# Rotated cross attention in a four-layer decoder: the keys' projection moves into the layer before, the inverse roots to ScalarE, all rotations to VectorE

## The chip, the cores and the metric

One core of one Trainium2 chip runs the whole kernel. The metric is the device time of one execution in microseconds. Its matrix engine is TensorE (PE in the profile, PEld for its weight loads), its vector engine VectorE (DVE), its activation engine ScalarE (ACT), the general one GpSimd (POOL); SyncE (SP) issues the transfers. SBUF is the on-chip memory, PSUM the accumulators that TensorE writes, eight banks of 512 fp32 per partition.

## The reference

The reference is a decoder on x of shape (8, 128, 128): eight sequences of 128 positions and 128 features. It has four layers, each of self attention, cross attention to a context and a feed-forward part. The change is in the first layer's cross attention, with 16 heads of 8 features:

```python
x = x + _L0_attn_ref(_layernorm(x), ...)
# cross attention: q from the normalized x, k and v from ctx_1024
q = rope(rms_norm(heads(_layernorm(x) @ Wq.T), q_norm_w))
k = rope(rms_norm(heads(ctx @ Wk.T), k_norm_w))
v = heads(ctx @ Wv.T)
x = x + (softmax(q k^T * 8**-0.5) v) @ Wo.T
# rms_norm over the 8 features of a head, eps 1e-10; rope turns
# feature i and i+4 of a head by the cosine and sine of its position
```

The keys and values depend on the context alone, so they can be computed before x is ready. The block ahead of it (L0a, the first layer's self attention) is a gated, quantized recurrence: x is normalized, rounded, multiplied by ternary weights, passed through an exponential, a logarithm and another exponential, normalized and rounded again, and projected.

## The kernel before

The eight sequences are held in two groups of four (g is 0 and 1). Each group has its own SBUF tiles and its own four PSUM banks. The program of each engine is written once per group as a generator that yields a pair (layer, phase) ahead of each piece of work; `weave` always runs the piece with the smallest pair, group 0 first on a tie. So the phase numbers fix the order of the instructions on each engine, and nothing is reordered on the chip. Engines wait for each other by semaphores (`wait_ge` on a named step). The layers are named L0a (attention), L0x (cross attention), L0f (feed-forward) and so on.

In L0a, VectorE computes the sums of the recurrence (L1362), then two mean squares per group (L1369 to L1373, "ms1" and "ms2"), whose inverse roots GpSimd takes as a power (L327, one instruction per group and root), and then the scales of the rounding (L1386 to L1392). After that come the transposes (L429), ScalarE's copy to bf16 (L929), the clamp (L1395), the projection and the residual sum into x (L1400).

In L0x:
- PE waits for x of L0a, projects keys into bank 1 and values into bank 2 from the transposed context (16 matmuls), transposes the normalized x and projects the queries.
- ACT copies the values (L867) and the transposed x (L856), squares queries and keys (L935) and copies the raw keys to the tile td (L856).
- DVE sums the squares per head (L1411), and takes the inverse roots of queries and keys together, 128 numbers per partition, by a shift, a constant and three rounds of Newton's method (L1413 to L1424, twelve instructions per group). It scales the queries (L1427) and rotates them (L1180, L1183 twice, L1185) into tc.
- POOL scales the keys (L356) and rotates them (L361, L363 twice, L365) into td, beside DVE.
- PE transposes both (L429), ACT copies them to QT and KT (L856), and the first masked keys are made by DVE (L1208) and POOL (L341).

Then the attention runs in 8 units per group: PE writes the mask (L413, ps<-bt) and the scores (L413, ps<-KTm,qk), DVE takes maxima (L1220) and subtracts (L1226), PE transposes (L476), ACT takes exponentials (L876), PE multiplies by the values. The code that the change touches:

## Time and profile before

| quantity | value |
|---|---|
| median of three runs | 748.72 us (747.66 to 748.99) |
| profiled execution | 747.51 us, of which its span is 745.7 us |
| mean granted clock of TensorE | 0.887 of full speed |
| PE busy | 597.0 us (80%) |
| DVE busy | 474.7 us (64%) |
| ACT busy | 249.3 us (33%) |
| POOL busy | 119.3 us (16%) |
| chain that ended last | PE 69%, DVE 23%, POOL 4%, ACT 2%, issue 2% |

The busy time of an engine is an average over stages of very different kinds; the chain names, at each moment, the work for which everything later waited. The granted clock has two levels, 0.5 (1.2 GHz) and 1.0 (2.4 GHz). The stretch around the change runs from 45 to 105 us of the span.

### The profile page before, as it was taken

What the parts mean: (1) busy time and instruction counts of PE and PEld (TensorE: products, weight loads), DVE (VectorE), ACT (ScalarE), POOL (GpSimd) and SP (SyncE); (2) the same over time, 40 slices, a digit from 0 to 9 for tenths busy, and PEclk for the clock granted to TensorE, in tenths of its full rate; (3) what the DMA queues carried; (4) which work ended last, traced back from release to release, by engine and by line L of the source; (5) the groups of instructions that cost most, each with busy time, mean ns of one, the idle gap of its engine ahead of it and who ended that gap; (6) DMA issues with size and microseconds to landing.
All of it is one profiled execution on the core that took longest, in us unless ns stands there. A gap on an engine that the chain in (4) does not pass through costs nothing.

```text
span 745.7 us, 10768 instructions
## 1 busy us (share of the span) xinstructions
PE 597.0 (80%) x4297; PEld 391.0 (52%) x4297; DVE 474.7 (64%) x1212; ACT 249.3 (33%) x371; POOL 119.3 (16%) x118
## 2 busy tenths in 40 slices
PE   1414599977899889969987679999779958998567
PEld 1314255667455646556765646456435654556425
DVE  7788867677587567754344634875554455876585
ACT  2342124415334333424323342344221022443261
POOL 5022611013220041000002014100200043102020
PEclk9657579979899999997998899999799986999879
DMA  9700000000000000000000000000000000000000
GB/s 298 304 0 1 0 1 1 2 1 2 0 1 2 1 1 2 1 1 1 1 0 1 1 0 1 1 2 1 1 0 1 0 1 0 2 1 1 1 0 29
DMA packets 6721, 12.41 MB, mean 17 GB/s; under 512 B 528, under 2 KB 4880, under 8 KB 6288
## 3 DMA queue, kind: packets, MB, share of 16 engines
q1 hardware_dynamic: 6672, 11.73, 4.4%
q8 instruction: 34, 0.56, 0.3%
q14 instruction: 15, 0.12, 0.1%
HBM read 11.21 MB, written 0.52 MB: 16 GB/s over the span
## 4 chain that ended last, share of the span: by engine, by line
PE 69%; DVE 23%; POOL 4%; ACT 2%; issue 2%; DVEq 0%; ACTq 0%; POOLq 0%
PE ps L413 52%; PE ps L476 11%; PE ps L429 3%; DVE st L1121 2%; PE ps L495 2%; DVE xn L1309 2%; POOL rs L327 2%; DVE mx L1220 2%; DVE big L1226 2%; DVE mv L1124 1%; DVE x L1239 1%; PE ps L585 1%; ACT big L876 1%; DVE big L1451 1%; DVE s L1449 1%
## 5 line engine op out<-in xcount | busy, mean ns | idle before, releaser
L1220 DVE TENSOR_REDUCE mx<-ps 128x8 f32<-128x1024 f32 x80 | 98.0, 1224 | 58.8 <-PE ps L413 58.7
L876 ACT ACTIVATE big<-ps 128x1024 f32<-128x1024 f32 x80 | 81.9, 1024 | 129.3 <-PE ps L476 129.3
L1226 DVE TENSOR_TENSOR big<-ps,mx 128x1024 f32<-128x1024 f32 x80 | 98.0, 1225 | 6.9
L476 PE MATMUL ps<-kt,big 128*128 128x128 f32 x640 | 90.9, 287 | 7.0 <-DVE big L1226 6.9
L413 PE MATMUL ps<-KTm,qk 32*128 32x512 f32 x320 | 95.6, 677 | 0.0
L327 POOL TENSOR_TENSOR rs<-ve,negh 128x4 f32<-128x4 f32 x26 | 26.6, 1024 | 411.7 <-DVE ve L1126 411.6
L476 PEld LDWEIGHTS ps<-kt,big 128*128 128x128 f32 x640 | 71.4, 145 | 35.0 <-DVE big L1226 18.5
L413 PE MATMUL ps<-xnT,wt 128*128 128x512 f32 (+1 forms) x148 | 78.8, 672 | 3.1 <-DVE big L1496 3.1
L413 PEld LDWEIGHTS ps<-wt,big 128*128 128x128 f32 (+1 forms) x480 | 56.0, 191 | 9.2 <-issue 9.1
L413 PE MATMUL ps<-wt,big 128*128 128x128 f32 (+1 forms) x480 | 59.8, 279 | 0.0
L413 PEld LDWEIGHTS ps<-big,vaug 128*32 128x32 f32 x1280 | 30.4, 109 | 48.0 <-ACT big L876 45.5
L341 POOL TENSOR_TENSOR KTm<-qk,kt 128x512 f32<-128x512 f32 x34 | 37.6, 1114 | 104.4 <-PE ps L413 93.4
L413 PE MATMUL ps<-big,vaug 128*32 128x128 f32 x1280 | 50.5, 278 | 0.0
L413 PE MATMUL ps<-bt 128*128 128x512 bf16 (+1 forms) x192 | 48.6, 364 | 0.0
L429 PE MATMUL ps<-kt,xn 128*128 128x128 f32 x80 | 18.4, 373 | 36.9 <-DVE xn L1309 36.5
L413 PEld LDWEIGHTS ps<-xnT,wt 128*128 128x128 f32 (+1 forms) x148 | 29.4, 214 | 32.4 <-issue 27.3
L856 ACT ACTIVATE xnT<-ps 128x512 f32<-128x512 f32 x30 | 17.9, 598 | 80.1 <-PE ps L429 69.8
L413 PEld LDWEIGHTS ps<-KTm,qk 32*128 32x128 f32 x320 | 25.4, 194 | 35.4 <-issue 32.5
L1285 DVE SCALAR_TENSOR_TENSOR x<-ps,gw,x 128x128 f32<-128x128 f32 x80 | 22.3, 344 | 30.3 <-PE ps L413 29.5
L413 PEld LDWEIGHTS ps<-wt,xnT 128*128 128x128 f32 x256 | 37.4, 232 | 3.3 <-issue 2.7
L413 PE MATMUL ps<-wt,xnT 128*128 128x128 f32 (+2 forms) x256 | 37.6, 308 | 0.2 <-ACT xnT L856 0.2
L429 PEld LDWEIGHTS ps<-kt,xn 128*128 128x128 f32 x80 | 12.0, 187 | 41.7 <-issue 31.1
(273 smaller groups left out, 783.4 us busy)
## 6 DMA issues: line engine op xcount, KB each, us to landing
wt<-in_weights SPq DMA_DIRECT2D x1, 1664.0 KB, 17.0
wt<-in_weights SPq DMA_DIRECT2D x1, 1603.0 KB, 11.9
wt<-in_weights SPq DMA_DIRECT2D x6, 256.0 KB, 11.2
bt<-in_bconsts SPq DMA_DIRECT2D x1, 1024.0 KB, 8.5
rowt<-in_rows SPq DMA_DIRECT2D x1, 975.0 KB, 6.6
wt<-in_weights SPq DMA_DIRECT2D x1, 832.0 KB, 13.5
wt<-in_weights SPq DMA_DIRECT2D x1, 608.0 KB, 18.0
wt<-in_weights SPq DMA_DIRECT2D x1, 580.0 KB, 5.5
```

The lines of the kernel that those rows point to most:

```text
L327: pool.tensor_tensor(out, src, negh[:, :], ALU.pow).then_inc(*s.step(name + "_r"))
L341: pool.tensor_tensor(t.KTm[:, b % 2, :, :], keys_of(t, b), own_head(), ALU.mult).then_inc(*s.step(f"keys{b}"))
L413: return pe.matmul(out, lhsT, rhs, start=start, stop=stop, **k)
L429: ins = pe.transpose(seq(bk, b), src[:, b, :], ident)
L476: ins = pe.transpose(heads_of(pair(g, u))[:, j // HG, j % HG, :], pr[:, (u % 2) * HH + j, :], ident)
L495: ins = pe.transpose(out, t.ot[b][:, i * P:(i + 1) * P], ident)
L856: act.activation(out, src, ACT.Copy).then_inc(*s.step(name))
L876: act.activation(half, heads_of(pair(g, u)), ACT.Exp, scale=SCALES[l]).then_inc(*s.step(f"exp{u}"))
L1121: dve.bn_stats(t.st[:, b, :], src[:, b, :]).then_inc(*s.step())
L1220: dve.tensor_reduce(top, S, AX.X, ALU.max).then_inc(*s.step())
L1226: dve.tensor_tensor(pr[:, half * HH:(half + 1) * HH, :].rearrange("p (i j) k -> p i j k", i=2), S, top.unsqueeze(3).to_broadcast([P, 2, HG ...
L1285: dve.scalar_tensor_tensor(x[:, b, :], bank(banks[e])[:, b * P:(b + 1) * P], gw[:, b, e:e + 1], x[:, b, :], ALU.mult, ALU.add).then_inc(*s ...
```

## The change

The changed kernel moves the key projection of L0x into the end of L0a, at phase 12.5, into bank 2. It waits there for the step ms1, after which bank 2 has been read. ACT squares and copies the raw keys there as well, and DVE sums the squares. In L0x the value projection waits only for that copy instead of for x. The inverse roots are computed by ACT as exp(-0.5 * ln(sum/8 + 1e-10)), one logarithm and one exponential per group for the keys (phase 0.2 and 0.4) and for the queries (phase 6). DVE rotates the keys too: group 0's ahead of the queries, group 1's after them. The queries are rotated from PSUM first and scaled afterwards. Group 0's keys are transposed early; the others at their old place. POOL waits for both groups' rotated queries before it spreads keys. The first masked keys are made at phase 7 instead of 19. The last attention layer (L3a) keeps its form. Declarations of a constant and of tiles are cut from the diff.

```diff
...
@@ -335,2 +337,5 @@
                         pool.wait_ge(*s.at(f"{l}.KT"))
+                        if l == "L0x":
+                            for other in range(GROUPS):
+                                pool.wait_ge(*s.at("L0x.qrot", other))
                         if first == 0:
@@ -352,10 +357,3 @@
                 pool.wait_ge(*s.at(f"{l}.kraw"))
-                if l == "L0x":
-                    pool.wait_ge(*p.at("pre.gwT"))
-                    pool.wait_ge(*s.at("L0x.y2"))
-                    pool.tensor_tensor(raw, new, t.y2[:, heads:2 * heads].unsqueeze(2).to_broadcast([P, heads, HD]), ALU.mult).then_inc(*s.step())
-                    pool.wait_ge(*s.last())
-                    cos, sin, one, two = cw[1][:, :], sw[1][:, :], slice(0, HD // 2), slice(HD // 2, HD)
-                else:
-                    cos, sin, one, two = const("c3"), const("s3"), slice(0, HD, 2), slice(1, HD, 2)
+                cos, sin, one, two = const("c3"), const("s3"), slice(0, HD, 2), slice(1, HD, 2)
                 pool.tensor_tensor(new, raw, cos.unsqueeze(1).to_broadcast([P, heads, HD]), ALU.mult).then_inc(*s.step())
@@ -391,3 +389,3 @@
                     rsqrt(t.rs[:, :], t.ve[:, :], "var2")
-                if l in ("L0x", "L3a"):
+                if l == "L3a":
                     yield from rotate_keys(n, l)
@@ -542,2 +540,8 @@
+            def turn_keys():
+
+                pe.wait_ge(*s.at("L0a.x"))
+                pe.wait_ge(*s.at("L0x.krot"))
+                turn_rows(1, t.td, "KTp")
+
             def turn_gates(n, l, k):
@@ -566,4 +570,3 @@
                     if l == "L0x":
-                        pe.wait_ge(*s.at("L0a.x"))
-                        project_rows(1, ctxT, w("L0x_wk"), "k")
+                        pe.wait_ge(*s.at("L0a.kraw"))
                     else:
@@ -602,4 +605,9 @@
                         pe.transpose(bank(3)[:, 0:E2], gwn[:, :], ident[0:E2, 0:E2]).then_inc(*p.step("gwTp"))
-                    yield n, 14
+                    yield n, 12.5
                     pe.wait_ge(*s.at("L0a.ctxT"))
+                    if g == 0:
+                        pe.wait_ge(loaded["L0x"], 16)
+                    pe.wait_ge(*s.at("L0a.ms1"))
+                    project_rows(2, ctxT, w("L0x_wk"), "k")
+                    yield n, 14
                     if g == GROUPS - 1:
@@ -621,2 +629,5 @@
                         project_rows(2, xnT, w("L3a_wv"), "v")
+                    if l == "L0x" and g == 0:
+                        yield n, 6
+                        turn_keys()
                     yield n, 8
@@ -624,4 +635,7 @@
                     turn_rows(0, t.tc, "QTp")
-                    pe.wait_ge(*s.at(f"{l}.krot"))
-                    turn_rows(1, t.td, "KTp")
+                    if l == "L3a":
+                        pe.wait_ge(*s.at("L3a.krot"))
+                        turn_rows(1, t.td, "KTp")
+                    elif g == GROUPS - 1:
+                        turn_keys()
                     yield n, 20
@@ -863,2 +877,14 @@
+            def logarithm(m, need):
+
+                part = slice(m * GB * H, (m + 1) * GB * H)
+                act.wait_ge(*s.at(need))
+                act.activation(t.y2[:, part], t.v2[:, part], ACT.Ln, bias=tiny[:, 0:1], scale=1.0 / HD).then_inc(*s.step("log"))
+
+            def inverse_root(m, name):
+
+                part = slice(m * GB * H, (m + 1) * GB * H)
+                act.wait_ge(*s.last())
+                act.activation(t.y2[:, part], t.y2[:, part], ACT.Exp, scale=-0.5).then_inc(*s.step(name))
+
             def values():
@@ -897,2 +923,6 @@
                 if l == "L0x":
+                    yield n, 0.2
+                    logarithm(1, "L0a.kv")
+                    yield n, 0.4
+                    inverse_root(1, "kroot")
                     yield n, 1
@@ -924,2 +954,6 @@
                     act.activation(tc[:, :, :], tc[:, :, :], ACT.Exp, scale=-float(P)).then_inc(*s.step("f128"))
+                    yield n, 12.5
+                    act.wait_ge(*s.at("L0a.k"))
+                    act.activation(t.ta[:, GB:2 * GB, :], four(bank(2)), ACT.Square).then_inc(*s.step("ksq"))
+                    read(t.td[:, :, :], four(bank(2)), "k", "kraw")
                     yield n, 13
@@ -932,6 +966,7 @@
                     if l == "L0x":
-                        for m, nm in ((1, "k"), (0, "q")):
-                            act.wait_ge(*s.at(f"L0x.{nm}"))
-                            act.activation(t.ta[:, m * GB:m * GB + GB, :], four(bank(m)), ACT.Square).then_inc(*s.step(f"{nm}sq"))
-                        read(t.td[:, :, :], four(bank(1)), "k", "kraw")
+                        act.wait_ge(*s.at("L0x.q"))
+                        act.activation(t.ta[:, 0:GB, :], four(bank(0)), ACT.Square).then_inc(*s.step("qsq"))
+                        yield n, 6
+                        logarithm(0, "L0x.qv")
+                        inverse_root(0, "qroot")
                     if l == "L3a":
@@ -940,4 +975,7 @@
                     yield n, 9
+                    if l == "L0x" and g == 0:
+                        read(KT, bank(1), "KTp", "KT")
                     read(QT, bank(0), "QTp", "QT")
-                    read(KT, bank(1), "KTp", "KT")
+                    if l == "L3a" or g == GROUPS - 1:
+                        read(KT, bank(1), "KTp", "KT")
                     yield from attend(n, l)
@@ -1174,2 +1212,7 @@
+            def mean_of_heads(m, name):
+
+                part = t.v2[:, m * GB * H:(m + 1) * GB * H]
+                dve.tensor_reduce(part, ta[:, m * GB:m * GB + GB, :].rearrange("p b (h d) -> p (b h) d", h=H), AX.X, ALU.add).then_inc(*s.step(name))
+
             def rotate(v, cos, sin, out, name, swap):
@@ -1187,2 +1230,6 @@
+            def first_keys(l):
+                dve.wait_ge(*s.at(f"{l}.KT"))
+                dve.tensor_tensor(t.KTm[:, 0, :, :], keys_of(t, 0), own_head(), ALU.mult).then_inc(*s.step("keys0"))
+
             def attend(n, l):
@@ -1204,6 +1251,5 @@
-                if l in ("L0x", "L1a", "L3a"):
+                if l in ("L1a", "L3a"):
                     yield n, 19
-                    dve.wait_ge(*s.at(f"{l}.KT"))
-                    dve.tensor_tensor(t.KTm[:, 0, :, :], keys_of(t, 0), own_head(), ALU.mult).then_inc(*s.step("keys0"))
+                    first_keys(l)
                 if l in ("L1x", "L2x"):
@@ -1383,2 +1429,5 @@
                     variance_of(outer, 1e-8, "ms2")
+                    yield n, 12.5
+                    dve.wait_ge(*s.at("L0a.ksq"))
+                    mean_of_heads(1, "kv")
                     yield n, 13
@@ -1403,28 +1452,25 @@
                 if l == "L0x":
+                    def rotate_keys():
+                        raw = ta[:, GB:2 * GB, :].rearrange("p b (h d) -> p (b h) d", h=H)
+                        dve.wait_ge(*s.at("L0x.kroot"))
+                        dve.tensor_tensor(raw, td[:, :, :].rearrange("p b (h d) -> p (b h) d", h=H),
+                                          wide(t.y2[:, GB * H:2 * GB * H], HD), ALU.mult).then_inc(*s.step())
+                        dve.wait_ge(*s.last())
+                        rotate(raw, cw[1][:, :], sw[1][:, :], td, "krot", "half")
-                    v2, y2, h2, hh = t.v2, t.y2, t.h2, GB * H
+                    if g == 0:
+                        yield n, 2
+                        rotate_keys()
                     yield n, 6
-                    dve.wait_ge(*s.last())
-                    for m, nm in ((0, "q"), (1, "k")):
-                        dve.wait_ge(*s.at(f"L0x.{nm}sq"))
-                        v = ta[:, m * GB:m * GB + GB, :].rearrange("p b (h d) -> p (b h) d", h=H)
-                        dve.tensor_reduce(v2[:, m * hh:(m + 1) * hh], v, AX.X, ALU.add).then_inc(*s.step())
-                    dve.wait_ge(*s.last())
-                    dve.tensor_scalar(v2[:, :], v2[:, :], 1.0 / HD, 1e-10, ALU.mult, ALU.add).then_inc(*s.step())
-                    dve.wait_ge(*s.last())
-                    dve.tensor_scalar(h2[:, :].bitcast(I32), v2[:, :].bitcast(I32), 1, None, ALU.logical_shift_right).then_inc(*s.step())
-                    dve.wait_ge(*s.last())
-                    dve.tensor_scalar(y2[:, :].bitcast(I32), h2[:, :].bitcast(I32), -1.0, float(0x5F3759DF), ALU.mult, ALU.add).then_inc(*s.step())
-                    dve.wait_ge(*s.last())
-                    for _ in range(3):
-                        dve.tensor_tensor(h2[:, :], y2[:, :], y2[:, :], ALU.mult).then_inc(*s.step())
-                        dve.wait_ge(*s.last())
-                        dve.scalar_tensor_tensor(h2[:, :], h2[:, :], -0.5, v2[:, :], ALU.mult, ALU.mult).then_inc(*s.step())
-                        dve.wait_ge(*s.last())
-                        dve.scalar_tensor_tensor(y2[:, :], h2[:, :], 1.5, y2[:, :], ALU.add, ALU.mult).then_inc(*s.step("y2"))
-                        dve.wait_ge(*s.last())
-                    v = ta[:, 0:GB, :].rearrange("p b (h d) -> p (b h) d", h=H)
-                    dve.tensor_tensor(v, bank(0).rearrange("p (h d) -> p h d", d=HD), wide(y2[:, 0:hh], HD), ALU.mult).then_inc(*s.step())
-                    dve.wait_ge(*s.last())
-                    rotate(v, cw[0][:, :], sw[0][:, :], tc, "qrot", "half")
+                    dve.wait_ge(*s.at("L0x.qsq"))
+                    mean_of_heads(0, "qv")
+                    yield n, (6.2 if g == 0 else 6.4)
+                    rotate(bank(0).rearrange("p (h d) -> p h d", d=HD), cw[0][:, :], sw[0][:, :], tc, "qraw", "half")
+                    dve.wait_ge(*s.at("L0x.qroot"))
+                    new = tc[:, :, :].rearrange("p b (h d) -> p (b h) d", h=H)
+                    dve.tensor_tensor(new, new, wide(t.y2[:, 0:GB * H], HD), ALU.mult).then_inc(*s.step("qrot"))
+                    if g == GROUPS - 1:
+                        rotate_keys()
+                    yield n, 7
+                    first_keys(l)
                 if l == "L3a":
```

**VectorE, where L0x begins.** The first fence is the kernel before, from group 1's normalized x to the end of the first Newton round of group 0; v2, h2 and y2 are sums, half values and roots, and the last digit is the group.

```order
L1309 TENSOR_SCALAR xn1<-x1,mv1,rs1 128x128 x4
L1411 TENSOR_REDUCE v20<-big0 128x64 x2
L1413 TENSOR_SCALAR v20<-v20 128x128
L1415 TENSOR_SCALAR h20<-v20 128x128
L1417 TENSOR_SCALAR y20<-h20 128x128
L1420 TENSOR_TENSOR h20<-y20 128x128
L1422 SCALAR_TENSOR_TENSOR h20<-h20,v20 128x128
L1424 SCALAR_TENSOR_TENSOR y20<-h20,y20 128x128
```

Two more such rounds, the scaling and the rotation of the queries follow, and then all of it again for group 1. The changed kernel has from the same place on (cw1 and sw1 are the cosines and sines of the keys, cw0 and sw0 those of the queries):

```order
L1355 TENSOR_SCALAR xn1<-x1,mv1,rs1 128x128 x4
L1456 TENSOR_TENSOR big0<-td0,y20 128x512
L1223 TENSOR_TENSOR td0<-big0,cw1 128x512
L1226 TENSOR_TENSOR big0<-big0,sw1 128x64x4 x2
L1228 TENSOR_TENSOR td0<-td0,big0 128x512
L1216 TENSOR_REDUCE v20<-big0 128x64
L1216 TENSOR_REDUCE v21<-big1 128x64
L1223 TENSOR_TENSOR tc0<-ps,cw0 128x512
L1226 TENSOR_TENSOR big0<-ps,sw0 128x64x4 x2
L1228 TENSOR_TENSOR tc0<-tc0,big0 128x512
L1471 TENSOR_TENSOR tc0<-tc0,y20 128x512
L1223 TENSOR_TENSOR tc1<-ps,cw0 128x512
```

The twelve small instructions of each group are gone; four instructions of group 0's key rotation and its scaling stand in front of the queries' sums. Group 1's keys come behind group 1's queries:

```order
L1226 TENSOR_TENSOR big1<-ps,sw0 128x64x4 x2
L1228 TENSOR_TENSOR tc1<-tc1,big1 128x512
L1471 TENSOR_TENSOR tc1<-tc1,y21 128x512
L1456 TENSOR_TENSOR big1<-td1,y21 128x512
L1223 TENSOR_TENSOR td1<-big1,cw1 128x512
L1226 TENSOR_TENSOR big1<-big1,sw1 128x64x4 x2
L1228 TENSOR_TENSOR td1<-td1,big1 128x512
L1233 TENSOR_TENSOR KTm0<-qk0,kt 128x512
L1233 TENSOR_TENSOR KTm1<-qk1,kt 128x512
```

What moved is the whole key rotation, from POOL to DVE, and the scaling of the queries, from ahead of the rotation to behind it.

**ScalarE, from the end of L0a to the transposed keys.** Before, from the last rounding on (the semaphore each waits for is in brackets):

```order
L929 ACTIVATE qk0<-ps,magic 128x512 [waits L0a_tensor0]
L929 ACTIVATE qk1<-ps,magic 128x512 [waits L0a_tensor1]
L867 ACTIVATE vaug0<-ps 128x64x8 [waits L0x_tensor0]
L867 ACTIVATE vaug1<-ps 128x64x8 [waits L0x_tensor1]
L856 ACTIVATE xnT0<-ps 128x512 [waits L0x_tensor0]
L856 ACTIVATE xnT1<-ps 128x512 [waits L0x_tensor1]
L935 ACTIVATE big0<-ps 128x512 [waits L0x_tensor0] x2
L856 ACTIVATE td0<-ps 128x512 [waits L0x_tensor0]
L935 ACTIVATE big1<-ps 128x512 [waits L0x_tensor1] x2
L856 ACTIVATE td1<-ps 128x512 [waits L0x_tensor1]
L856 ACTIVATE qk0<-ps 128x512 [waits L0x_tensor0] x2
L856 ACTIVATE qk1<-ps 128x512 [waits L0x_tensor1] x2
```

In the changed kernel from the copy of group 1's transposed x on:

```order
L870 ACTIVATE xnT1<-ps 128x512 [waits L0x_tensor1]
L968 ACTIVATE big0<-ps 128x512 [waits L0x_tensor0]
L968 ACTIVATE big1<-ps 128x512 [waits L0x_tensor1]
L882 ACT_TABLE_LOAD
L882 ACTIVATE y20<-v20,tiny 128x64 [waits L0x_vector0]
L888 ACT_TABLE_LOAD
L888 ACTIVATE y20<-y20 128x64 [waits L0x_scalar0]
L882 ACT_TABLE_LOAD
L882 ACTIVATE y21<-v21,tiny 128x64 [waits L0x_vector1]
L888 ACT_TABLE_LOAD
L888 ACTIVATE y21<-y21 128x64 [waits L0x_scalar1]
L870 ACTIVATE qk0<-ps 128x512 [waits L0x_tensor0] x2
```

Each logarithm and each exponential has a table load ahead of it; the loads themselves carry no wait. The keys' roots stand ahead of the value copies: a load, the logarithms of both groups, a load, the exponentials of both groups.

**TensorE, from the gate transposition in L0a.** Before:

```order
L602 MATMUL ps<-kt,gwn 128x16
L429 MATMUL ps<-kt,big0 128x128 x4
L429 MATMUL ps<-kt,big1 128x128 x4
L413 MATMUL ps<-wtern,qk0 128x128 x4
L413 MATMUL ps<-wtern,qk1 128x128 x4
L413 MATMUL ps<-wt,ctxT0 128x128 x8
L413 MATMUL ps<-wt,ctxT1 128x128 x8
```

After:

```order
L605 MATMUL ps<-kt,gwn 128x16
L411 MATMUL ps<-wt,ctxT0 128x128 x4
L411 MATMUL ps<-wt,ctxT1 128x128 x4
L427 MATMUL ps<-kt,big0 128x128 x4
L427 MATMUL ps<-kt,big1 128x128 x4
L411 MATMUL ps<-wtern,qk0 128x128 x4
L411 MATMUL ps<-wtern,qk1 128x128 x4
L411 MATMUL ps<-wt,ctxT0 128x128 x4
L411 MATMUL ps<-wt,ctxT1 128x128 x4
```

Four matmuls per group, the key projection, moved from behind x of L0a to ahead of the last transposes of L0a.

## Rows read from the trace of the kernel before

**Rows 1.** The page: busy time by engine; the copies of ScalarE.
```profile
PE 597.0 (80%) x4297; PEld 391.0 (52%) x4297; DVE 474.7 (64%) x1212; ACT 249.3 (33%) x371; POOL 119.3 (16%) x118
...
L856 ACT ACTIVATE xnT<-ps 128x512 f32<-128x512 f32 x30 | 17.9, 598 | 80.1 <-PE ps L429 69.8
```

**Rows 2.** Chain of waits, 0:160; columns: start us, us, what.
```profile
88.35 5.83 PE ps L413 x12
94.19 1.90 PE ps L476 x8
...
98.94 1.90 PE ps L476 x8
...
104.02 2.06 PE ps L413 x22
106.08 1.03 PE ps L476 x8
```

**Rows 3.** Timeline of DVE, 43:100; columns: start, us, engine, line, operation, [idle before].
```profile
45.73 0.17 DVE L1373 TENSOR_SCALAR s<-s 128x4 f32<-128x4 f32 x1
...
49.42 0.17 DVE L1373 TENSOR_SCALAR s<-s 128x4 f32<-128x4 f32 x1
49.81 0.16 DVE L1386 TENSOR_TENSOR s<-s,s4b 128x4 f32<-128x4 f32 x1 [0.22 <-POOL s4b L327]
```

**Rows 4.** Timeline of DVE, further on: normalization, roots and rotation of group 0.
```profile
60.96 2.36 DVE L1309 TENSOR_SCALAR xn<-x,mv,rs 128x128 f32<-128x128 f32 x8
66.09 1.28 DVE L1411 TENSOR_REDUCE v<-big 128x64 f32<-128x512 f32 x2 [2.76 <-ACT big L935]
...
71.12 0.69 DVE L1427 TENSOR_TENSOR big<-ps,y 128x512 f32<-128x512 f32 x1
71.85 1.03 DVE L1180 TENSOR_TENSOR tc<-big,cw 128x512 f32<-128x512 f32 x1
72.80 2.23 DVE L1183 TENSOR_TENSOR big<-big,sw 128x256 f32<-128x256 f32 x2
...
76.08 1.28 DVE L1411 TENSOR_REDUCE v<-big 128x64 f32<-128x512 f32 x2
```

**Rows 5.** Timeline of PE, 43:100.
```profile
51.80 1.09 PE L429 MATMUL ps<-kt,big 128*128 128x128 f32 x4 [15.48 <-DVE big L1160]
...
57.40 5.62 PE L413 MATMUL ps<-wt,ctxT 128*128 128x128 f32 x32 [0.64 <-DVE x L1400]
62.85 1.19 PE L429 MATMUL ps<-kt,xn 128*128 128x128 f32 x8
64.19 2.05 PE L413 MATMUL ps<-wt,xnT 128*128 128x128 f32 x16 [0.15 <-ACT xnT L856]
```

**Rows 6.** Timeline of ACT, 36:45.
```profile
41.76 1.28 ACT L924 ACT_TABLE_LOAD   x1
43.06 1.15 ACT L924 ACTIVATE tc<-tc 128x512 f32<-128x512 f32 x2
```

**Rows 7.** Timeline of POOL, 43:100: the first operation of a key rotation.
```profile
71.26 1.07 POOL L356 TENSOR_TENSOR big<-td,y 128x512 f32<-128x512 f32 x1 [9.09 <-DVE y L1424]
```

**Rows 8.** Timeline of DVE, 590:640: a rotation in the last attention layer.
```profile
605.60 0.69 DVE L1180 TENSOR_TENSOR tc<-ps,kt 128x512 f32<-128x512 f32 x1 [2.99 <-PE ps L413]
606.20 0.75 DVE L1183 TENSOR_TENSOR big<-ps,kt 128x256 f32<-128x256 f32 x2
606.99 0.69 DVE L1185 TENSOR_TENSOR tc<-tc,big 128x512 f32<-128x512 f32 x1
```

**Rows 9.** Timeline of ACT, 600:622.
```profile
618.51 1.28 ACT L876 ACT_TABLE_LOAD   x1
```

**Rows 10.** Stretches; columns: window, length, busy PE PEld DVE ACT POOL, PEclk, DMA share, GB/s.
```profile
57.50:61.00 3.50, 3.50 (x17) 3.50 (x18) 3.40 (x23) 0.00 (x0) 1.01 (x1) 0.50 0.03 7
61.50:66.50 5.00, 4.59 (x38) 4.00 (x36) 2.11 (x8) 3.50 (x8) 0.67 (x1) 1.00 0.00 0
```

**Rows 11.** Line L959: small exponentials on ACT, ns min/median/max.
```profile
L959 ACT ACTIVATE lgm<-lgm x4: 222/226/231, 161.6 to 343.0; 128x32 f32<-128x32 f32 x2, 128x24 f32<-128x24 f32 x2
```

6 lines of the change are left out of this document (4 added, 2 removed).

## The prediction

> **What bounds the kernel now.** I read the page first: PE is the busiest engine with 597.0 us, DVE has 474.7 us [rows 1]. That says nothing of the stretch that is changed, so the chain of waits came next, and there I looked for the last moment that the change can move. It is 88.35 us, the end of the last key transposition, after which PE works without a pause into the attention [rows 2]. Everything behind it is in the same order in both kernels, so what the change gives is the shift of this one point, unless the clock of PE changes what follows. Then the timeline of each engine between 45 and 88 us, to see what each wait ends on. DVE finishes the normalized x at 63.32 us (60.96 + 2.36), sits idle 2.76 us for ScalarE's squares, starts group 0's roots at 66.09 and group 1's at 76.08, so a group costs 9.99 us of DVE, and two take it to 86.1 [rows 4]. Two transpositions of 1.12 us close the gap to 88.35 [rows 2]. DVE therefore bounds the stretch; PE and ACT wait for it.
>
> **A group's 9.99 us before.** The sums of squares take 1.28 us for two tensors. From 67.40 (the row of 66.09 plus its 1.28 and the handoff) to 71.12 run the twelve Newton instructions, 3.75 us. The scaling is 0.69 us, and from 71.85 to 76.08 the rotation takes 4.23 us [rows 4]. The same rotation in the last attention layer, from 605.60 to 607.68, takes 2.08 us, with 0.75 us for the two half products that take 2.23 us here [rows 4, 8]. The difference of 2.15 us falls in the time in which POOL rotates the keys, which starts at 71.26 [rows 7]. I read it as the two engines hindering each other in SBUF.
>
> **What is added in L0a.** PE sat idle 15.48 us until 51.80, so the key projection has room there [rows 5]. It may start at 45.9, when group 0's ms1 is written [rows 3]. Sixteen matmuls (32 records) took 5.62 us from 57.40; eight took 2.05 us from 64.19, 0.26 us each [rows 5]. The clock was 0.50 until 61.0 and 1.00 from 61.5 [rows 10]. With 1.8 us of the 5.62 at 0.26 us, nine matmuls are left for 3.8 us at the low clock, 0.43 us each. Four cost 1.7 us, so group 1's keys are there at 49.4. ACT's square takes 0.6 us (598 ns for the same copy) [rows 1], to 50.1. DVE has ms2 at 49.59 and its next instruction stood at 49.81 [rows 3]. Now two sums of 0.64 us come between. The second waits until 50.1 at most, and ends at 50.95. So L0a ends 1.16 us later. At the high clock it would be 1.1 us, with 0.6 us per matmul 1.9 us. ACT's four instructions end by 50.8, before 51.80, when the first rounded tile was transposed [rows 5].
>
> **What leaves L0x's front.** The values are projected while DVE adds x, and PE no longer carries the keys. This gives nothing by itself: the normalized x ends at 63.32 and its last transposition could hardly end sooner than it did, 62.85 + 1.19 = 64.04 [rows 4, 5]. The key roots stand on ACT before the value copies: two loads of 1.28 us and four small activations of 0.25 us (226 ns for 24 to 32 numbers) [rows 6, 11], 3.6 us. ACT can begin them when its last copy of L0a is done, which was before 57.40, and is 1.16 us later now, and so ends them by 62.2. The first transposed x comes at 64 or later: free.
>
> **The new path through DVE**, with 0.03 us between instructions. It starts 1.16 us late, at 64.5.
> - Group 0's keys: scaling 0.72, rotation 2.1 (the price of rows 8, since POOL does nothing in this stretch), to 67.35. Under it PE transposes x (to 65.1), ACT copies (to 65.8), PE projects both groups' queries (to 66.2 and 67.2), ACT squares them (66.9 and 67.85).
> - The queries' sums: 0.65 each, 68.0 and 68.7. They no longer wait, so the 2.76 us of idleness is filled.
> - Rotation of group 0's queries from PSUM: to 70.8. Meanwhile ACT takes the root. Its table load needs no operand, and in the last layer a load ran right behind the copy at 617.90, ahead of its exponential's wait [rows 9]. So: load from 67.9 to 69.2, logarithm 69.45, load 70.75, exponential 71.0. DVE waits 0.3 us, scales to 71.8.
> - Group 1's queries: rotation to 73.9, root at 71.0 + 2 x 1.55 = 74.1, scaling to 74.9.
> - Group 1's keys: 2.85 us, to 77.75. POOL may spread group 0's second keys from 75 on, one operation of about 1.1 us. Its four operations cost DVE 2.15 us in some 5 us, so I add 0.55, to 78.3. The ends are 0 and 1.1.
> - One transposition of 1.12 us: 79.5 instead of 88.35.
>
> The Trainium skill, page "SBUF — State Buffer", section "Who interferes with whom", says that of a DVE instruction with two SBUF inputs and a GpSimd one that reads SBUF, the one issued second blocks for the other's whole length. By it the last term could be 1.1 instead of 0.55 us; the trace agrees as far as two half products took 2.23 us beside POOL and 0.75 without.
>
> **The sum.** Before, from the normalized x: 2.77 + 9.99 + 9.98 + 2.24 = 25.0 us. After: 15.0 us. Less 10.0, plus 1.16 in L0a: 8.8 us less. The profiled execution took 747.51 us, so it becomes 738.7. The median of the three runs, 748.72, lies 1.2 us above, which gives **739.9 us**.
>
> **Rivals.**
> 1. *The queries are projected at the low clock.* Before, PE had worked from 57.40 without a pause when the clock rose about 61.2 [rows 5, 10]. Now it has only eight matmuls and then a gap of 2 us. If the clock stays low, the last transposition costs 0.5 us more and the projections 1.7 us each instead of 1.0, so group 1's squares come at 69.65, and its sums end at 70.3 instead of 68.7: 1.6 us later at the end, 741.5 us. For it speaks the gap, against it that 4 us of work still stand ahead of it.
> 2. *The clock in the attention.* There a unit cost 4.75 us (94.19 to 98.94) at first, and 3.09 us (2.06 + 1.03) later [rows 2]. The change to the fast rate came about 14 us after 88.35. One unit earlier gives 1.65 us more: 738.2.
> 3. *The halves cost that much without POOL too.* Then the layout, halves of four read from SBUF, and not the neighbour is what makes the rotation slow. The key rotations would cost 4.25 each: 4.3 us more, 744.2 us. Against it: the last sum of a rotation has the same layout in both layers, and took 1.0 us here (75.03, the end of the half products, to 76.05) and 0.69 us there [rows 4, 8].
> 4. *A table switch costs twice its row.* It would be 2.6 us each if it also had to wait for the engine to drain. The queries' roots then come at 73.6 and 79.3, the keys' end moves to 83.5 and the transposition to 84.6: only 3.75 us less, 745.0. Against it: from the load at 41.76 to the exponential at 43.06 lie 1.30 us [rows 6]. The Trainium skill, page "ScalarE: Activation LUTs", section "What ACT_TABLE_LOAD costs", states 1283 ns and a drain of about 1380 ns for every switch; by its figure an estimate of the whole is this rival's. The load's own length agrees with the trace, a drain is not seen there.
> 5. *Slower than before: the attention stays at the low clock.* The place is the first units of the scores. The transposes that precede them now come scattered, at 67, 72, 75 and 78 us, with DVE's work between. If the clock rose not after three cold units but later, each one costs 1.65 us. From six more units (9.9 us) on, the kernel is slower than before; with eight it is 753 us. For it: before, PE was busy in all of 88 to 102 and the clock still stayed low. Against it: those units themselves did raise it, and they are unchanged.
>
> **How the numbers follow.** My forecast 0.58, rival 1 0.16, rival 2 0.11, rival 3 0.05, rival 4 0.05, rival 5 0.03, a gain lost in other ways 0.02. Two parts in a thousand, 1.5 us, are about what a measurement of this kernel can tell from no change. All but the last two are beyond that: faster 0.95, within it 0.02, slower 0.03. The range goes from 737.6 (a unit earlier, no contention) to 743.0 (rival 1 with both dear ends, 0.7 in L0a and 0.55 at POOL); rivals 3 to 5 lie outside.
>
> **What would show it.** In the changed trace: the first L0a scale instruction about 1.2 us later; no idleness of DVE ahead of the queries' sums beyond 0.1 us; all rotations near 2.1 us; ACT's load, logarithm, load, exponential in 3.1 us per group; the first mask matmul at 79.5. Wrong would be a DVE wait for ACT of more than 1 us at the scaling, half products over 0.5 us with POOL idle, or a start of the attention after 82.

## The result and the profile after

The changed kernel takes 739.36 us (738.49 to 741.1 in 4 runs) against 748.19 us (746.02 to 748.99) of the kernel before in the same comparison: a ratio of 0.9889, with a 95% interval of 0.9861 to 0.9918. The prediction was 739.9 us. The profiled execution took 739.54 us with a span of 737.7 us, 8.0 us less than before; the prediction had 738.7 us for it. Busy time went from DVE (474.7 to 468.7 us) and POOL (119.3 to 107.7) to ACT (249.3 to 259.2), as the page shows:

```profile
PE 597.4 (81%) x4289; PEld 392.3 (53%) x4297; DVE 468.7 (64%) x1198; ACT 259.2 (35%) x385; POOL 107.7 (15%) x109
```

The chain of waits around the start of the attention (start us, us, what) answers to [rows 2]:

```profile
79.68 1.09 PE ps L427 x4
80.77 5.84 PE ps L411 x12
86.61 1.90 PE ps L474 x8
...
91.37 1.90 PE ps L474 x8
...
95.24 1.03 PE ps L474 x8
...
98.33 1.02 PE ps L474 x8
```

The start of the attention stands at 80.77 instead of 88.35, 7.6 us earlier. This execution was already 0.26 us later than the one of before when group 0's ms1 was written, which lies ahead of everything that the change touches (45.99 against 45.73 in [rows 3]), so the change moved the start by 7.8 us; 8.8 were predicted. From there on the two are alike: a unit costs 4.76 us (86.61 to 91.37) at first and 3.09 us (95.24 to 98.33) later, and the fast rate comes 13 to 14 us after the start in both.

DVE after the change answers to [rows 3] and [rows 4] (start, us, engine, line, operation, count, idle before it and what ended it):

```profile
49.76 0.68 DVE L1216 TENSOR_REDUCE v<-big 128x64 f32<-128x512 f32 x1
50.74 0.69 DVE L1216 TENSOR_REDUCE v<-big 128x64 f32<-128x512 f32 x1 [0.30 <-ACT big L957]
51.34 0.15 DVE L1435 TENSOR_TENSOR s<-s,s4b 128x4 f32<-128x4 f32 x1
...
64.60 0.69 DVE L1456 TENSOR_TENSOR big<-td,y 128x512 f32<-128x512 f32 x1
...
68.05 1.51 DVE L1216 TENSOR_REDUCE v<-big 128x64 f32<-128x512 f32 x2 [0.64 <-ACT big L968]
...
72.17 0.69 DVE L1471 TENSOR_TENSOR tc<-tc,y 128x512 f32<-128x512 f32 x1 [0.62 <-ACT y L888]
...
75.40 0.69 DVE L1471 TENSOR_TENSOR tc<-tc,y 128x512 f32<-128x512 f32 x1 [0.55 <-ACT y L888]
76.01 0.69 DVE L1456 TENSOR_TENSOR big<-td,y 128x512 f32<-128x512 f32 x1
76.73 1.41 DVE L1223 TENSOR_TENSOR td<-big,cw 128x512 f32<-128x512 f32 x1
```

The path is the predicted one, with four kinds of small loss on it: the sums in L0a (the scale instruction stands at 51.34 instead of 49.81), a wait of 0.64 us for ScalarE's squares ahead of 68.05, one wait for each root, and one product of 1.41 us that takes 0.69 elsewhere. Beside that product POOL spreads the first keys:

```profile
76.27 1.33 POOL L346 TENSOR_TENSOR KTm<-qk,kt 128x512 f32<-128x512 f32 x1 [12.73 <-ACT qk L870]
```

ScalarE's roots of the queries, with table loads as long as those of [rows 6] and [rows 9]:

```profile
68.25 0.60 ACT L968 ACTIVATE big<-ps 128x512 f32<-128x512 f32 x1 [0.30 <-PE ps L411]
68.86 1.28 ACT L882 ACT_TABLE_LOAD   x1
70.16 0.35 ACT L882 ACTIVATE y<-v,tiny 128x64 f32<-128x64 f32 x1
70.52 1.28 ACT L888 ACT_TABLE_LOAD   x1
71.82 0.26 ACT L888 ACTIVATE y<-y 128x64 f32<-128x64 f32 x1
72.09 1.28 ACT L882 ACT_TABLE_LOAD   x1
```

A load lasts 1.28 us and the next activation starts 0.01 to 0.02 us behind it. A group costs 3.23 us (68.86 to 72.09), where the prediction had 3.1. The granted clock by stretch answers to [rows 10] (window, length, busy PE, PEld, DVE, ACT, POOL, granted clock, DMA share, GB/s):

```profile
57.80:61.00 3.20, 3.20 (x18) 3.20 (x16) 3.10 (x17) 3.16 (x7) 0.00 (x0) 0.50 0.03 8
61.00:66.50 5.50, 3.51 (x15) 2.81 (x15) 5.30 (x22) 1.94 (x4) 2.04 (x2) 0.50 0.00 0
66.50:71.00 4.50, 2.15 (x17) 1.91 (x16) 3.65 (x8) 3.30 (x5) 0.00 (x0) 0.95 0.00 0
```

Before, the clock was 1.00 from 61.5 to 66.5. Now PE has a pause of 1.86 us ahead of the first transposition of x (63.49), and its clock is 0.50 until 66.5.

### The profile page after: what moved, and what is told of

Read it like the earlier page. It is cut to its first block, busy times and chain, and to the rows that moved or that the text cites. A ratio compares the mean times of both kernels' runs of the same rounds, so it can differ in the third digit from the quotient of the medians.

```text
span 737.7 us, 10755 instructions
## 1 busy us (share of the span) xinstructions
PE 597.4 (81%) x4289; PEld 392.3 (53%) x4297; DVE 468.7 (64%) x1198; ACT 259.2 (35%) x385; POOL 107.7 (15%) x109
## 4 chain that ended last, share of the span: by engine, by line
PE 69%; DVE 20%; ACT 3%; POOL 3%; issue 2%; DMA 1%; SPq 1%; DVEq 0%; ACTq 0%
PE ps L411 52%; PE ps L474 11%; PE ps L427 3%; DVE st L1159 3%; PE ps L493 2%; DVE xn L1355 2%; POOL rs L329 2%; DVE big L1272 2%; DVE mx L1266 2%; DMA co<-in_ctx 1%; DVE mv L1162 1%; DVE x L1285 1%; PE ps L588 1%; ACT big L902 1%; DVE s L1495 1%
## 5 line engine op out<-in xcount | busy, mean ns | idle before, releaser
L411 PE MATMUL ps<-bt 128*128 128x512 bf16 (+1 forms) x184 | 46.9, 364 | 0.6 <-issue 0.2
L427 PEld LDWEIGHTS ps<-kt,xn 128*128 128x128 f32 x80 | 12.5, 194 | 44.2 <-issue 31.1
```

What stands on the lines that cost most here:

```text
L411: return pe.matmul(out, lhsT, rhs, start=start, stop=stop, **k)
L427: ins = pe.transpose(seq(bk, b), src[:, b, :], ident)
```

## The experiments

"Start" is the end of group 1's last key transposition, from which PE works on into the attention. The repairs of e5 to e8 move it by about a microsecond or less each, while the executions of one kernel differ by 2 to 11 us (737.42 to 739.29 in e5, 735.96 to 746.54 in e4). So the start and the local rows decide, and the totals are given beside them. Totals are medians, ratios are to the kernel before.

Each start is read from the one profiled execution of its kernel, and these executions differ ahead of the change as well. The last column takes that out: it is the start less the moment at which group 0's ms1 was written.

| kernel | profiled execution, us | ms1 of group 0 | start | start less ms1 |
|---|---|---|---|---|
| before | 747.51 | 45.73 | 88.35 | 42.62 |
| changed | 739.54 | 45.99 | 80.77 | 34.78 |
| e1 | 755.34 | 45.69 | 89.79 | 44.10 |
| e2 | 745.71 | 46.59 | 88.02 | 41.43 |
| e3 | 743.18 | 46.01 | 85.78 | 39.77 |
| e4 | 746.54 | 45.80 | 80.98 | 35.18 |
| e5 | 738.53 | 45.75 | 79.50 | 33.75 |
| e6 | 736.57 | 45.74 | 79.74 | 34.00 |
| e7 | 742.24 | 45.90 | 79.79 | 33.89 |
| e8 | 740.51 | 45.82 | 80.40 | 34.58 |
| e9 | 736.19 | 45.82 | 76.68 | 30.86 |
| e10 | 731.74 | 45.91 | 75.73 | 29.82 |
| e11 | 739.07 | 46.09 | 79.99 | 33.90 |
| e12 | 731.45 | 46.10 | 76.49 | 30.39 |

The profiled executions of e1 and e4 took 7 to 8 us more than their medians, those of e10 and e12 are the fastest of their kernels.

**e1: the move of the key rotation alone.** The kernel before, with POOL's scaling and rotation of the keys in L0x written on DVE behind the queries'.

```diff
-                if l in ("L0x", "L3a"):
+                if l == "L3a":
                     yield from rotate_keys(n, l)        # POOL
...
                     rotate(v, cw[0][:, :], sw[0][:, :], tc, "qrot", "half")
+                    dve.wait_ge(*s.at("L0x.kraw"))
+                    dve.tensor_tensor(raw, td..., wide(y2[:, hh:2 * hh], HD), ALU.mult).then_inc(*s.step())
+                    rotate(raw, cw[1][:, :], sw[1][:, :], td, "krot", "half")
```

> The kernel before with one part of the change: the key rotation of L0x moves from POOL to DVE, behind each group's query rotation; Newton roots and the late key projection stay. Theory (the slow rotations of before, 4.23 us, were due to POOL working beside them): every rotation now takes 2.1 us. A group costs DVE 1.28 + 3.75 + 0.72 + 2.1 + 2.85 = 10.7 us instead of 9.99, so the attention starts at about 88.7 us instead of 88.35, and the time is that of before, +0.3 us. Rival (the layout of halves read from SBUF is slow by itself): rotations stay near 4.2 us, the attention starts at about 97, +8 us.

Measured: 748.15 us, ratio 1.0019 (0.9984 to 1.0054); start at 89.8, where 88.7 was expected.

```profile
72.24 0.69 DVE L1180 TENSOR_TENSOR tc<-big,cw 128x512 f32<-128x512 f32 x1
72.85 0.75 DVE L1183 TENSOR_TENSOR big<-big,sw 128x256 f32<-128x256 f32 x2
73.63 0.69 DVE L1185 TENSOR_TENSOR tc<-tc,big 128x512 f32<-128x512 f32 x1
```

The same instructions in the same layout took 1.03, 2.23 and 1.0 us in [rows 4]. With POOL idle they are at the price of [rows 8]: the neighbour was the cause, and rival 3 falls. Each key rotation on POOL thus cost DVE 2.1 us in its own rotation, and one on DVE costs 2.85 us with its scaling, so the move alone gives nothing. The start is 1.1 us later than expected: a key spreading of POOL, from 79.05 to 80.16, stretched the Newton instruction issued at 79.30 from 0.29 to 1.01 us, and the queries' squares came 0.4 us later.

**e2: ScalarE's roots alone.** The kernel before with the twelve Newton instructions replaced.

```diff
-                    dve.tensor_scalar(v2[:, :], v2[:, :], 1.0 / HD, 1e-10, ALU.mult, ALU.add)...
...
+                        act.wait_ge(*s.at("L0x.sums"))
+                        act.activation(t.y2[:, :], t.v2[:, :], ACT.Ln, bias=tiny[:, 0:1], scale=1.0 / HD)...
+                        act.activation(t.y2[:, :], t.y2[:, :], ACT.Exp, scale=-0.5)...
```

> The kernel before with another part alone: the inverse roots of queries and keys by ACT (load, logarithm, load, exponential on 128 numbers per partition, per group), DVE waiting for them. Theory (a root costs DVE the wait, and DVE has nothing else to do in this order): group 0's first load can begin at 67.95 only, behind ACT's copies, so its root is there at 71.2, as late as Newton's; group 1's takes 2.0 us behind its sums instead of 3.75. The attention starts at about 86.6, -1.75 us against before. Rival (a switch of tables costs 2.6 us): start at 92 or later, +3 us.

Measured: 745.14 us, ratio 0.9962 (0.9938 to 0.9985); start at 88.0, which is 87.1 without the 0.9 us by which this execution was late ahead of the change; 86.6 was expected.

```profile
72.52 0.69 DVE L1422 TENSOR_TENSOR big<-ps,y 128x512 f32<-128x512 f32 x1 [4.02 <-ACT y L943]
73.25 0.96 DVE L1187 TENSOR_TENSOR tc<-big,cw 128x512 f32<-128x512 f32 x1
74.13 2.23 DVE L1190 TENSOR_TENSOR big<-big,sw 128x256 f32<-128x256 f32 x2
...
80.86 0.69 DVE L1422 TENSOR_TENSOR big<-ps,y 128x512 f32<-128x512 f32 x1 [2.16 <-ACT y L943]
```

In this order DVE waits 4.02 and 2.16 us for the roots that Newton's method took 3.75 us to make. The second wait is shorter since the load had run ahead of the logarithm's wait, as ScalarE's rows show:

```profile
72.44 1.28 ACT L941 ACT_TABLE_LOAD   x1
78.73 0.40 ACT L941 ACTIVATE y<-v,tiny 128x128 f32<-128x128 f32 x1 [5.01 <-DVE v L1418]
```

The half products are back at 2.23 us, with POOL beside them. A switch costs one load of 1.28 us (the logarithm that follows the load at 69.10 starts at 70.40), and rival 4 falls.

**e3: the queries' roots by Newton's method** in the changed kernel, twelve instructions on 64 numbers in place of `logarithm(0, ...)` and `inverse_root(0, ...)`:

```diff
-                        logarithm(0, "L0x.qv")
-                        inverse_root(0, "qroot")
...
                     mean_of_heads(0, "qv")
+                    ... 3 + 3 x 3 instructions on v2, h2, y2 [:, 0:GB * H]
```

> The changed kernel with the queries' roots by Newton on DVE again (twelve instructions on 64 numbers per partition, per group), the keys' roots still on ACT. Theory (with the sums in front, ACT's roots are hidden beside the rotations, and only waits of 0.6 us remained): 2 x 2.9 us of Newton come in, 1.17 us of waits go, the attention starts at 85.4 instead of 80.77, +4.6 us against the changed kernel. Rival (ACT's roots gave nothing, the gain came from the other parts): start within 1 us of 80.77.

Measured: 744.59 us, ratio 0.9958 (0.9923 to 0.9992); start at 85.8, 5.0 us later than in the changed kernel. The twelve instructions took 3.0 us (68.81 to 71.84); twice that is 6.0 us, less the waits for the roots. So 5.0 of the 7.8 us are that the queries' roots leave DVE *and* have a rotation to hide under: alone, the rotations on DVE (e1) made the start 1.5 us later and the roots on ScalarE (e2) 1.2 us earlier. The other 2.8 us belong to the rest of the change. By the rows, the early key projection gives DVE a key rotation to do where it was idle for 2.76 us, but no run takes that projection out alone, so its share is argued and not shown.

**e4: both key rotations on POOL**, in the changed order.

```diff
-                if l == "L3a":
+                if l in ("L0x", "L3a"):
                     yield from rotate_keys(n, l)        # POOL, after L0x.kroot
...
-                    if g == 0:
-                        yield n, 2
-                        rotate_keys()                   # DVE, and the same for the other group
```

> The changed kernel with both key rotations on POOL again, from the early roots of ACT (ready at 60.7). POOL is free from 63.5, so it turns group 0's keys to about 69.3 and group 1's to 75.1, while DVE has only the queries. Theory (a POOL rotation costs DVE about half of POOL's time while both work, and DVE waits for ACT anyway): the queries end near 76.8, two transpositions behind it, start of the attention at 79.0, 1.8 us better than the changed kernel. Rival (each query rotation costs 4.2 us again beside POOL): queries end at 78.6, start at 80.8, no difference.

Measured: 738.44 us, ratio 0.9852 (0.979 to 0.9914); start at 81.0, where 79.0 was expected. The rival had 80.8, from query rotations of 4.2 us. Both missed the mechanism:

```profile
62.23 4.81 DVE L1362 TENSOR_SCALAR xn<-x,mv,rs 128x128 f32<-128x128 f32 x8
```

The eight normalizations take 4.81 instead of 2.36 us. POOL starts on the keys at 63.41 and keeps at it; the normalizations ahead of that moment are at their usual 0.34 us, and the one issued at 64.48 takes 1.42 us. The queries' rotations, which ran later, were at 2.1 us even where POOL's last operation (71.90, 1.27 us) lay beside their first, which reads PSUM. DVE is rid of 5.7 us of key rotations, and now waits 3.5 us for the squares of the queries, which the later x holds back.

**e5: the sums over the squared keys late in L0a**, in DVE's gap ahead of the clamp; those of both groups, though the expectation of e9 speaks of group 1's.

```diff
-                    yield n, 12.5
-                    dve.wait_ge(*s.at("L0a.ksq"))
-                    mean_of_heads(1, "kv")
...
+                    yield n, 14.9
+                    dve.wait_ge(*s.at("L0a.ksq"))
+                    mean_of_heads(1, "kv")
```

> The changed kernel with the sums of the keys' squares on DVE moved from phase 12.5 of L0a to 14.9, into the gap in which DVE waits 0.28 and 1.30 us for ACT. Theory (in the changed kernel DVE's two sums and the wait for the second one put 1.5 us on the path of L0a: 49.81 became 51.34): they become free, the scale chain of L0a starts 1.3 us earlier and the attention at 79.4 instead of 80.77. Rival (the path of L0a's end runs through ACT's four key instructions or through PE): less than 0.5 us of it arrives.

Measured: 738.85 us, ratio 0.9858 (0.9814 to 0.9903); start at 79.5, 1.27 us earlier than in the changed kernel, or 1.03 us without what this execution was early ahead of the change.

```profile
49.83 0.16 DVE L1432 TENSOR_TENSOR s<-s,s4b 128x4 f32<-128x4 f32 x1 [0.22 <-POOL s4b L329]
...
53.69 1.27 DVE L1216 TENSOR_REDUCE v<-big 128x64 f32<-128x512 f32 x2
```

The scale instruction is back where [rows 3] has it, and the sums fill a gap. In L0a the repair is worth 1.27 us (from ms1 to the scale instruction it is 5.35 us in the changed kernel and 4.08 here); the start gets 1.03 of it. The term of L0a was real and avoidable.

**e6: both logarithms ahead of both exponentials**, one phase number each, and both rotations ahead of both scalings.

```diff
                         logarithm(0, "L0x.qv")
+                        yield n, 6.5
                         inverse_root(0, "qroot")
...
+                    yield n, 6.6
                     dve.wait_ge(*s.at("L0x.qroot"))
```

> The changed kernel with the queries' roots paired: logarithms of both groups behind one table load, then the exponentials of both behind another, and DVE rotates both groups' queries before it scales them. Two table loads fewer. Theory (DVE's waits of 0.62 and 0.55 us at the scaling come from ACT's four loads): both waits go, less one 0.03 gap; the attention starts 1.0 us earlier, at 79.8. Rival (the wait is ACT's handoff and not the loads): no difference.

Measured: 737.9 us, ratio 0.9858 (0.9809 to 0.9906); start at 79.7, 1.0 us earlier, or 0.8 us counted from ms1.

```profile
73.77 1.29 DVE L1473 TENSOR_TENSOR tc<-tc,y 128x512 f32<-128x512 f32 x2
```

ScalarE has two loads instead of four, and no wait stands at the scalings.

**e7: four needless matmuls after the values**, in PE's pause ahead of the normalized x.

```diff
                     project_rows(2, ctxT, w(f"{l}_wv"), "v")
+                    if l == "L0x" and g == GROUPS - 1:
+                        for b in range(GB):
+                            ins = mm(seq(3, b), ctxT[:, b * P:(b + 1) * P], w("L0x_wv"))
```

> The changed kernel with four more matmuls of PE behind group 1's value projection (the same products once more, into a bank that nobody reads before the next transposition overwrites it). They close PE's idle time of 1.86 us before the transposition of x. Theory (the queries were projected partly at the low clock because PE had stopped): the clock is at 1.0 before 63.5, the transpositions cost 0.6 and the projections 1.0 us each, ACT's second square ends near 67.6 instead of 68.85, and the attention starts 1.2 us earlier, at 79.5. Rival (the clock rises when it rises, or DVE's key rotation bounds this place anyway): start within 0.4 us of 80.77.

Measured: 739.26 us, ratio 0.9861 (0.9817 to 0.9905); start at 79.8, 1.0 us earlier, or 0.9 us counted from ms1.

```profile
65.21 2.01 PE L411 MATMUL ps<-wt,xnT 128*128 128x128 f32 x16
...
67.42 1.28 DVE L1220 TENSOR_REDUCE v<-big 128x64 f32<-128x512 f32 x2
```

The first row is PE's projection of the queries (2.56 us in the changed kernel), the second DVE's sums, of another answer of the same trace, now without a wait. The clock was 1.00 from 64 on here and 0.50 until 66.5 in the changed kernel. Needless work made the kernel's start earlier: rival 1's mechanism was at work in the changed kernel, at some 0.7 to 0.9 us.

**e8: POOL's first spread waits for group 1's rotated keys.**

```diff
                                 pool.wait_ge(*s.at("L0x.qrot", other))
+                            pool.wait_ge(*s.at("L0x.krot", 1))
```

> The changed kernel with one wait more: POOL spreads group 0's second keys only when group 1's keys are rotated. Theory (the one instruction of the rotation that took 1.41 instead of 0.69 us was held up by POOL's 1.33 us beside it): it takes 0.69 us, and the attention starts 0.7 us earlier, at 80.05. Rival (the 1.41 us is something of DVE's own): no difference.

Measured: 738.74 us, ratio 0.9855 (0.981 to 0.99); start at 80.4, where 80.05 was expected; counted from ms1 it is 0.2 us earlier than in the changed kernel and not 0.7. The queries' sums ended 0.3 us later, which the edit doesn't touch: PE projected the queries in 2.97 instead of 2.56 us, at a clock of 0.57 instead of 0.77 between 66 and 68.

```profile
77.08 0.69 DVE L1224 TENSOR_TENSOR td<-big,cw 128x512 f32<-128x512 f32 x1
```

The product is at 0.69 instead of 1.41 us. In the changed kernel it was issued at 76.73, while POOL's operation ran until 77.60, and ended at 78.14: it was held up for 0.72 of the 0.87 us that POOL had left. The Trainium skill, page "SBUF — State Buffer", section "Who interferes with whom", says that the later one waits until the earlier is through; this row agrees, nearly. The row of e10 does not show the whole length: there a sum issued at 71.19, when POOL's operation had 0.39 us left, paid 0.25 us.

**e9: all four together** (e5 to e8).

> All four repairs in one kernel: group 1's key sums late in L0a, both logarithms ahead of both exponentials, POOL's first spread after the rotated keys, and four matmuls between the values and the queries. Theory, that each loss was a term of its own on one path: the attention started at 80.77 in the changed kernel, less 1.27 (sums), 1.03 (logarithms), 0.98 (clock) and 0.72 (POOL), so it starts at 76.8, and the kernel takes 739.4 less 4.0, 735.4 us. Rival, that the repairs share a loss: the earlier x of the late sums makes ScalarE's squares or roots the last thing to come, and the start stays at 77.8 or later, 736.4 us or more.

Measured: 736.63 us, ratio 0.9873 (0.9844 to 0.9902). PE (start, us, engine, line, operation, count, idle before):

```profile
72.18 1.97 PE L428 MATMUL ps<-kt,tc 128*128 128x128 f32 x8 [5.42 <-DVE tc L1478]
75.59 1.08 PE L428 MATMUL ps<-kt,td 128*128 128x128 f32 x4 [1.45 <-DVE td L1234]
```

The start is at 76.7, 4.1 us earlier than in the changed kernel (3.9 from ms1), where 76.8 was expected and the rival had 77.8 or later. By the start the terms add up, and the rival falls. The time does not decide: it is 2.7 us less, not 4.0, and 736.63 us also meets the rival's 736.4 us or more. Six executions between 734.89 and 742.35 us can't tell the two apart.

**e10: e9, and group 1's keys rotated by POOL, after DVE's group 0.**

```diff
+                    pool.wait_ge(*s.at("L0x.kroot"))
+                    pool.wait_ge(*s.at("L0x.krot", 0))
...
-                if l == "L3a":
+                if l == "L3a" or l == "L0x" and g == GROUPS - 1:
                     yield from rotate_keys(n, l)        # POOL
```

> The combined kernel, and group 1's key rotation on POOL, begun only when DVE has rotated group 0's keys, so that no normalization or key work of DVE lies beside it. POOL's five operations take 1.2 us each, 6.0 us, from about 66 to 72.3, ahead of their use. DVE keeps only work on queries beside them, of which five instructions per group read PSUM or the table. Theory, that operands in PSUM keep DVE free of POOL: 2.85 us leave DVE's path and at most 0.5 per group come back at the last sum, so the attention starts at 74.2 to 74.9 instead of 76.8, and the kernel takes 732.8 to 733.5 us. Rival, that any DVE instruction that touches SBUF pays about 0.7 us beside POOL: five of them cost 3.5 us, the start stays at 77 or later, and nothing is gained over the combined kernel.

Measured: 732.71 us (731.74 to 735.54), ratio 0.9822 (0.9802 to 0.9843); start at 75.7.

```profile
67.29 0.68 DVE L1237 TENSOR_TENSOR tc<-ps,cw 128x512 f32<-128x512 f32 x1
67.89 0.75 DVE L1240 TENSOR_TENSOR big<-ps,sw 128x256 f32<-128x256 f32 x2
68.67 1.10 DVE L1242 TENSOR_TENSOR tc<-tc,big 128x512 f32<-128x512 f32 x1
```

With POOL busy from 66.23 to 71.58 beside them, the products that read PSUM are at their full speed (0.68 and 0.75 us), and the sum of two SBUF tiles pays 0.41 us, for group 1 0.25 us. That part of the theory is shown. But the start came only 1.0 us earlier than in e9, at 75.7 and not at 74.2 to 74.9. The chain of waits (start us, us, what) has PE in DVE's place now:

```profile
72.17 0.70 DVE tc L1486
72.92 2.82 PE ps L436 x12
```

All three sets of transpositions stand behind the scaling, at the low clock, 2.8 us; in e9 the two of the queries lay under DVE's key rotation. The time fell by 3.9 us, more than the start, and its 732.71 us meets the expected 732.8 to 733.5 by another cause than the expected one: the first units of the attention ran at the high clock:

```profile
76.00:80.00 4.00, 3.01 (x13) 0.75 (x11) 3.23 (x4) 0.37 (x1) 1.54 (x1) 1.00 0.00 0
```

**e11: PE's gaps ahead of the start filled**, in the changed kernel.

```diff
                         yield n, 6
                         turn_keys()
+                        for b in range(GB):
+                            for _ in range(2):
+                                ins = mm(seq(3, b), xnT[:, b * P:(b + 1) * P], w("L0x_wq"))
...                      # and the same behind group 0's turned queries
```

> The changed kernel with eight needless matmuls after the first keys' transposition and eight after group 0's queries', in PE's gaps of 4.3 and 2.2 us, so that PE works nearly without pause from 65.6 to 76. Their results are read by nothing. The attention starts at 80.8 as before, since DVE sets that. Question: what holds the clock at 0.50 in the attention's first 14 us. Theory, that it is the gaps ahead of the start: with them filled the clock is 1.00 at 80.8, three units cost 3.1 us instead of 4.75 and the first half unit as well, some 4.9 us less, 734.5 us. Rival, that the attention's own start (scores on 32 rows, with short pauses) holds it low whatever went before: the clock is 0.50 again a few us after 80.8, the gain is 0 to 1.5 us, 738 to 739.4 us.

Measured: 740.97 us, ratio 0.9919 (0.9903 to 0.9934); start at 80.0, where 80.8 was expected.

```profile
76.00:80.00 4.00, 1.75 (x12) 1.46 (x12) 3.84 (x6) 0.60 (x1) 1.27 (x1) 0.91 0.00 0
80.00:94.00 14.00, 14.00 (x40) 5.85 (x38) 8.04 (x7) 2.65 (x3) 2.59 (x2) 0.51 0.00 1
```

The clock was high up to the start and low right after it, for 14 us in which PE was busy all the time. As put, the theory falls and the rival holds. What the edit had left unfilled is the last pause, 2.25 us ahead of the last key transposition. This kernel with that pause filled as well was not run.

**e12: e9 with that last pause filled** by three matmuls.

```diff
                     elif g == GROUPS - 1:
+                        for b in range(GB - 1):
+                            ins = mm(seq(3, b), xnT[:, b * P:(b + 1) * P], w("L0x_wq"))
+                        ins.then_inc(*s.step("fill"))
                         turn_keys()
```

> The combined kernel with three needless matmuls between the queries' transpositions and group 1's keys', in the pause of 1.45 us that PE has there; at 0.43 us each they end at 75.4, so the start stays at 76.5 (up to 76.7). Their results are read by nothing. In the kernel with POOL rotating group 1's keys PE had no pause between 72.9 and 77.5, and the clock was 1.00 from about 76; in the combined kernel it paused from 74.15 to 75.59 and stayed at 0.50 to about 91.4. Theory, that this pause is what kept the clock down: it is 1.00 by 77 to 78, two to three units of 4.75 us become 3.1 us, and the kernel takes 736.6 less 3 to 5, 732 to 733.5 us. Rival, that something else decided it: the clock stays at 0.50 until 91 and the time is within 1 us of the combined kernel's, 736 to 737.5 us.

Measured: 733.2 us (731.45 to 738.59), ratio 0.9828 (0.9802 to 0.9854), 3.4 us less than e9, whose executions (734.89 to 742.35) and ratio (0.9844 to 0.9902) overlap with these; start at 76.5, as expected.

```profile
72.44 1.97 PE L428 MATMUL ps<-kt,tc 128*128 128x128 f32 x8 [5.42 <-DVE tc L1481]
74.21 1.48 PE L412 MATMUL ps<-wt,xnT 128*128 128x128 f32 x6
75.86 0.63 PE L428 MATMUL ps<-kt,td 128*128 128x128 f32 x4 [0.17 <-DVE td L1237]
76.33 0.59 PE L412 MATMUL ps<-bt 128*128 128x512 bf16 x2
76.85 1.13 PE L412 MATMUL ps<-KTm,qk 32*128 32x512 f32 x4
```

The transposition takes 0.63 instead of 1.08 us and the scores 1.13 instead of 2.08, from the first unit on. The clock and the median fit the theory, and the rival (0.50 until 91, 736 to 737.5 us) falls by the trace. That a pause there is what holds the clock down is not shown in general. The kernel before had none ahead of its last key transposition, and its clock stayed at 0.50 all the same:

```profile
86.11 1.12 PE L429 MATMUL ps<-kt,tc 128*128 128x128 f32 x4 [7.76 <-DVE tc L1185]
87.23 1.12 PE L429 MATMUL ps<-kt,td 128*128 128x128 f32 x4
```

Nor is the slow stretch behind the start of one length. By the granted clock it lasted 13 to 15 us in seven traces, but 8 us in e6, and 8.5 to 10 us in e1 to e4. In e6 the scores are fast from 88.0 on:

```profile
88.02 1.13 PE L411 MATMUL ps<-KTm,qk 32*128 32x512 f32 x4
```

e10 and e12 are the best versions found, some 14 us below the kernel before and 6 below the changed one.

## Why the prediction was right, point by point

- **The bound and the moment that moves.** Right. What the change gives is the shift of the start, 7.8 us, and the profiled executions differ by 8.0.
- **Rotations at 2.1 us without POOL** (rival 3 otherwise). Right, shown by e1.
- **A table switch costs its row** (rival 4 otherwise). Right, shown by e2 and by the four loads above. Its other half, that a load needs no operand, holds in e2 as well. The Trainium skill, page "ScalarE: Activation LUTs", section "What ACT_TABLE_LOAD costs", adds a drain of about 1380 ns; the load's 1.28 us agrees, and no row here shows the drain.
- **Sums in L0a: 1.16.** 1.27 us (51.34, less 0.26, less 49.81). e5 gives the 1.27 us back in L0a, and 1.03 us of it at the start.
- **Group 0's keys end at 67.35.** 67.41.
- **"They no longer wait" (the queries' sums).** This step failed in part. Predicted end 68.7, measured 69.48: a wait of 0.64 us, since PE transposed x and began to project the queries at the low clock, up to 66.5. Rival 1 had 70.3, so about half of it came true; e7 shows the mechanism. The argument against it, 4 us of work still ahead, weighed the work and not the pause of 1.86 us before it.
- **Waits for the roots, 0.3 and 0.2.** 0.62 and 0.55, some 0.4 us more at the end: the small logarithm took 0.35 us and not 0.25, and ScalarE's second square ended at 68.85 and not at 67.85.
- **POOL beside group 1's keys, 0.55 with ends 0 and 1.1.** 0.72 us on one instruction (e8).
- **Sum.** 79.5 predicted, 80.77 measured: 0.72 from the queries' squares, 0.38 from the roots, 0.16 from POOL, 0.10 from a later x (the execution's own offset of 0.26 us is more than that), less 0.09 in small differences.
- **The median came nearer than the path.** 739.36 against 739.9, though the path was 1.0 us longer than predicted. The profiled execution was 0.8 us above its forecast, and this time lay 0.2 us above its median, where that of before was 0.7 us below (748.19). Such agreement within a microsecond is luck. The prediction also took 1.5 us for what a measurement of this kernel can tell from no change; the 95% interval of this one is 2.1 us to either side, and those of the experiments are 1.2 to 4.6 us.
- **Rival 2 and rival 5, the clock in the attention.** Neither came in the profiled execution. Before and after, the slow stretch is 13 to 14 us. But in other traces it was as short as 8 us (e6), so a term of one to two units, 1.7 us each, stood outside the sum, and the 8.0 us between the two profiled executions match the shift because it was alike in both. e10 and e12 show that it can go altogether: their first units ran at the high clock from the start.
